# A drain between two stages reordered: probabilities, reciprocals and the first job's rounding

## What is computed

```python
q, k, v = heads(ln(x) @ Wq.T), heads(ln(x) @ Wk.T), heads(ln(x) @ Wv.T + bv)
a = softmax(q @ k.T * 384**-0.5 + adj)            # rows that are all zero give 0
x = x + (a @ v) @ Wo.T + bo
u = ln(x)
logits = u.mean(axis=1) @ router_w.T + router_b   # one choice for each graph
gate = softmax of the two greatest of four logits
h = act_e(u @ w1[e] + b1[e])                      # gelu, silu, mish, gelu
y = sum over the two experts of gate * (h @ w2[e] + b2[e]) + u
x = x + layernorm(y) * ln_g + ln_b
```

## Time and profile before

| what | us |
|---|---|
| median of 3 runs | 1617.83 |
| lowest, highest | 1617.38, 1619.46 |
| the profiled execution, its own time | 1619.34 |
| its span, first to last instruction | 1617.50 |
| TensorE busy | 1586.6 |
| VectorE busy | 1194.9 |
| ScalarE busy | 970.5 |
| GpSimd busy | 687.1 |

### The profile page before, as it was taken

The page is one execution under the profiler, slowest core; times in us unless marked ns, Lnnn a source line. Parts: engine busy times, 40 slices in busy tenths (PEclk is TensorE's granted clock), DMA queues, the critical chain, the costliest instruction groups (busy, mean ns, idle before and its releaser), DMA issues.

```text
span 1617.5 us, 44743 instructions
## 1 busy us (share of the span) xinstructions
PE 1586.6 (98%) x12720; PEld 1524.0 (94%) x12720; DVE 1194.9 (74%) x3754; ACT 970.5 (60%) x2880; POOL 687.1 (42%) x1105
## 2 busy tenths in 40 slices
PE   8999999999999999989999999999999999999998
PEld 7999999999999999879999999999999999999998
DVE  5787788878887778777766666676777767677776
ACT  6899999988999988863433333344344433344442
POOL 3777887778777877731111111111111111111112
PEclk9999999999999999999999999999999999999999
DMA  5433333344444433682211111111111111111211
GB/s 181 161 121 124 104 118 116 130 155 152 155 158 145 152 132 116 211 341 84 60 59 53 56 59 60 56 59 61 61 60 46 60 60 56 60 60 52 67 47 45
DMA packets 93512, 163.87 MB, mean 101 GB/s; under 512 B 10305, under 2 KB 73793, under 8 KB 92097
## 3 DMA queue, kind: packets, MB, share of 16 engines
q1 hardware_dynamic: 91664, 145.01, 27.2%
q10 hardware_dynamic: 1584, 15.73, 2.7%
HBM read 96.22 MB, written 64.49 MB: 99 GB/s over the span
## 4 chain that ended last, share of the span: by engine, by line
PE 89%; DVE 4%; ACT 2%; issue 2%; DMA 1%; DVEq 1%; POOL 0%; ACTq 0%; POOLq 0%; SPq 0%
PE bank L495 69%; PE bank L570 5%; PE bank L709 5%; PE bank L522 3%; PE bank L593 3%; PE bank L610 2%; PE bank L579 1%; PE bank L602 1%; DVE half_t L1458 1%; DVE inverse L1465 1%; DVE inverse L1461 1%; ACT inverse L1009 1%; ACT at_hi L1002 1%; ACT prob L781 1%; DVE hid L1339 0%
## 5 line engine op out<-in xcount | busy, mean ns | idle before, releaser
L495 PE MATMUL bank<-w_hi,ut_in 128*128 x1536 | 421.2, 341 | 0.4 <-issue 0.4
L495 PE MATMUL bank<-w_both,at_hi 128*128 x1524 | 390.0, 336 | 8.7 <-DVE at_lo L1430 8.0
L781 ACT ACTIVATE prob<-att,heads 128x128 f32<-128x128 f32 x768 | 297.5, 393 | 15.3 <-DVE heads L1182 12.3
L495 PEld LDWEIGHTS bank<-w_both,at_hi 128*128 128x128 f32 x1524 | 275.1, 188 | 14.3 <-issue 14.3
L495 PEld LDWEIGHTS bank<-w_hi,ut_in 128*128 128x128 f32 x1536 | 279.5, 188 | 1.4 <-issue 1.4
L495 PE MATMUL bank<-w_lo,ut_in 128*128 x768 | 256.9, 335 | 0.0
L495 PE MATMUL bank<-w_both,at_lo 128*128 x762 | 255.7, 336 | 0.0
L926 ACT ACTIVATE hid<-hid 128x384 f32<-128x384 f32 x192 | 95.1, 526 | 257.2 <-DVE hid L1339 256.5
L1002 ACT ACTIVATE at_hi<-bank,gate_col 128x384 fp32r<-128x384 f32 x254 | 133.4, 576 | 191.0 <-PE bank L709 189.1
L1158 POOL TENSOR_TENSOR xz<-xz,lnb_wide 128x384 f32<-128x384 f32 x64 | 67.6, 1057 | 405.6 <-DVE xz L1496 384.0
L1430 DVE SCALAR_TENSOR_TENSOR at_lo<-bank,gate_col,at_hi 128x384 fp32r<-128x384 f32 x254 | 144.8, 612 | 112.5 <-ACT at_hi L1002 112.5
(11 more groups left out here) (139 smaller groups left out, 3482.3 us busy)
## 6 DMA issues: line engine op xcount, KB each, us to landing
xu_scratch<-xu SPq DMA_DIRECT2D x64, 384.0 KB, 2.3
xz<-xu_scratch SPq DMA_DIRECT2D x64, 384.0 KB, 3.3
x_in<-in_x SPq DMA_DIRECT2D x32, 384.0 KB, 3.3
xu<-in_x SPq DMA_DIRECT2D x32, 384.0 KB, 4.3
ut_scratch<-ut_out SPq DMA_DIRECT2D x64, 192.0 KB, 1.9
ut_in<-ut_scratch SPq DMA_DIRECT2D x64, 192.0 KB, 2.3
out_dram<-xz SPq DMA_DIRECT2D x64, 192.0 KB, 1.9
w_lo<-in_L_ffn_w SPq DMA_DIRECT2D x4, 1152.0 KB, 6.1
```

Of the source, the lines that this page charges most:

```text
L495: last = nc.tensor.matmul(acc, lhs[c][a], rhs[c][b], start=start and n == 0, stop=stop and n == len(terms) - 1)
L781: nc.scalar.activation(prob[g][:, hh, :], att[g][:, head, :], ACT.Exp, bias=neg_max[g][:, head:head + 1], scale=-1.0, accum_out=row_sum[g] ...
```

## The change

In the drain, ScalarE copies one of the three groups of graph 62's probabilities between the exponentials of graph 63, and the reciprocals of graph 62 before the last three of them; VectorE's list loses that copy. TensorE's third group of transposes of graph 63 moves behind the output projection of graph 62. In the expert stage, ScalarE rounds the activation of job (0, 0) before it activates job (0, 1). All work stays, only its place and, for one copy, its engine change; all other steps and jobs are as before.

```diff
--- before.py
+++ after.py
@@ -662,9 +662,10 @@
                     transpose_u(B - 2)
                 if h == B:
 
-                    for c in range(PTC):
-                        transpose_probs(B - 1, c)
+                    transpose_probs(B - 1, 0)
+                    transpose_probs(B - 1, 1)
                     project_o(B - 2)
+                    transpose_probs(B - 1, 2)
                     spread_inverse(B - 1)
                     attend(B - 1)
                 if h < B:
@@ -969,8 +970,11 @@
 
             normalise_x1(B - 4)
             load_under_residuals()
-            exps(B - 1, (0, 1, 2, 3))
+            exps(B - 1, (0,))
+            take_probs(B - 2, 0)
+            exps(B - 1, (1, 2))
             take_inverse(B - 2)
+            exps(B - 1, (3,))
             load_under_scores()
             take_probs(B - 1, 0)
             take_probs(B - 1, 1)
@@ -1021,11 +1025,14 @@
                 for k in range(K):
                     if graph(b, 0):
                         e = choice(b, k)
+                        if isinstance(b, int) and (b, k) == (0, 1):
+
+                            split_act_hi(0, 0, 0)
                         if not isinstance(b, int) or (b, k) != (0, 0):
                             activate(b, k, e)
                     if k == 0 and graph(b, -1):
                         split_act_hi(b - 1, 1, m - 1)
-                    if k == 1 and graph(b, 0):
+                    if k == 1 and graph(b, 0) and not (isinstance(b, int) and b == 0):
                         split_act_hi(b, 0, m)
                     if isinstance(b, int) and (b, k) == (0, 1):
                         take_u(B - 1)
@@ -1399,7 +1406,7 @@
 
             add_bias_and_max(B - 1, (0, 1, 2, 3))
             invert_sums(B - 2)
-            for c in range(PTC):
+            for c in range(1, PTC):
                 take_probs(B - 2, c)
             residual(B - 3)
             divide(B - 2)
```

## The result

The changed kernel takes **1622.11 us** (median of 20 runs, 1620.03 to 1624.19), the kernel before, run beside it, 1618.86 us (20 runs, 1617.33 to 1619.48): 3.25 us more, ratio 1.0020, interval 1.0013 to 1.0027. The profiled execution took 1622.67 us (span 1620.9) against 1619.34. The forecast was 1618.6 us, with 1616.6 to 1621.0 as its range, so the kernel became slower than the range allows, by almost exactly the 0.2% that was called measurable. About 1 us of the gap to the forecast is the median of before itself: 1617.83 from three runs, 1618.86 from twenty. As a difference, +0.8 us was forecast and +3.25 measured. All that follows is about these 2.45 us.

A forecast was written before the change was run, and what follows sets the result against it. TensorE, busy 98% of the span, was taken as the bound, so only its waits could pay. -0.67 + 2.07 = +1.40 us, less 0.35 and 0.2, gave +0.8 with edit C 0: 1617.83 to 1618.6 us, range 1616.6 to 1621.0.

The forecast's parts named there:

- Edit B: Drain, graph 63's last transposes behind project_o(62): transposes, copy and inversion in a row add 2.07 us, passage 1.4 us later.
- Edit C: Expert stage, rounding job (0, 0) first: looks like 2.2 us, counted 0, hidden by w2 and then the Mish chain.
- w2's landing: Last piece of w2 lands at 719.76 us, taken as unchanged within 0.5 us; second layer starts at 720.1 as before.
- Edit A: Drain, ScalarE's copy and reciprocals between exponentials: reciprocals and the rest (L1247 before, L1248 after) come 0.67 us earlier.
- The Mish chain: Job (0, 1)'s activation, L1009 to L1469, ready at 725.91 us before; sets when TensorE's next first layer starts.
- The table load: ScalarE's activation table load in the drain: 1.28 us, ending at 704.6, adds nothing; even 2.66 us leaves the sum standing.
- +0.8 us: Delay of take_u, L1009, sum_nodes and all after: 1.40 at 705 us less 0.35 and 0.2, rounded.
- The 0.35 for the stored ut: ScalarE's idle time before the Mish chain, waiting for a stored ut, absorbs 0.35 us of the 1.40.
- The 0.2: Rounding first uses 0.2 us, between 0 and 0.4, of the 1.51 us ScalarE spent issuing before 715.85.
- Rival 1: Clock drops in new pauses at 704 to 706 or before 726, 1.8 us each: one fall 22%, two 7%.
- Rival 2: Drain follows the earlier reciprocals, inverse not held up by the copy: all 0.67 us earlier, 1617.1 us; 12%.
- rival 3: w2 there all along: second layer 2.2 us sooner with clock kept, at most 4.0 us gained, 1613.8 us; 3%.

The follow-up runs named there:

- changed_again: The changed kernel itself, unaltered, run and profiled once more; +3.09 us against the kernel before.
- order_alone: The kernel before with only the third group of transposes moved behind project_o(62); +2.73 us against the kernel before.
- inverse_first: The changed kernel, but VectorE inverts graph 63's sums before copying its third group of probabilities; +0.69 us against the kernel before.
- pause_filled: The changed kernel with 14 unused matmuls in TensorE's pause ahead of the Mish job's transposes; +2.55 us against the kernel before.
- all_filled: The changed kernel with unused matmuls in three TensorE pauses: 9 ahead of project_o(62), 8 behind the third transposes, 14 ahead of the Mish transposes; +1.69 us against before.
- round_first_alone: The kernel before with only job (0, 0)'s rounding put ahead of job (0, 1)'s activation; +0.44 us against the kernel before.
- order_undone: The changed kernel with TensorE's old order, all three groups of transposes before project_o(62); +0.94 us against the kernel before.
- best: Kernel before with edit A, Mish chain moved ahead, 13 unused matmuls before the w2 wait, take_u between Mish squares, early ut store; -0.54 us against before.
- best_filled: The run best with 6 more unused matmuls ahead of the third group of transposes; -0.50 us against the kernel before.
- drain_alone: The kernel before with only ScalarE's copy and graph 62's reciprocals put between the exponentials; +0.50 us against the kernel before.

## Why the prediction was wrong

**What held.** Edit B's chain: L579 came 1.32 us later by the common measure (+1.40 forecast), at 705.24 in the profile. Edit C gives nothing, since w2 is waited for instead: the second layer starts at 720.63, or 25.37 us behind the first exponential, against 25.48 before, so w2's landing did not move although its last issue came later. Edit A gave what it said at L1248 (0.67 us earlier by the common measure), but only inside the drain. The Mish chain sets (0, 1), with L1476 at +1.40. The table load never mattered: 704.13 + 1.28 = 705.41, and the copy behind it began at 705.83, with its idle time put down to the spreading:

```profile
704.13 1.28 ACT L985 ACT_TABLE_LOAD   x1 [1.53 <-PE bank L570]
705.83 0.49 ACT L812 ACTIVATE inv_t<-bank 128x384 f32<-128x384 f32 x1 [0.41 <-PE bank L579]
```

By the 2.66 us that the Trainium skill (ScalarE: Activation LUTs, section What ACT_TABLE_LOAD costs) gives for a switch with its drain, the copy could not have begun before 706.79 (an estimate: 704.13 + 2.66); the measurement decides. The prediction said that the rows of before can't exclude the 2.66 us. The trace of before does: there the load began 0.02 us after the instruction ahead of it had ended, and the copy behind it at 703.88, which is before 701.49 + 2.66 = 704.15.

**The first failed step: "+0.8 us" for the Mish chain.** It was mis-sized; 1.39 was measured at (0, 1). The two slacks were to absorb 0.35 and 0.2 of 1.40. The 0.35 for the stored ut was used. The 0.2 was not a slack but a loss: ScalarE spent 2.09 us issuing ahead of at_hi, not 1.51. Its chain holds two loads of a value into a register at L904, 0.72 and 0.47 us:

```profile
716.25 0.72 ACTq L904
...
717.54 0.47 ACTq L904
```

at_hi so began 23.08 us behind the first exponential and not at 22.4, and take_u, which was 25.39 behind it before, at 26.81: +1.42. The same loads took 0.08 and 0.47 in changed_again and 0.35 and 0.43 in order_alone. Why they vary is open, but the loss is no single event: the same stretch of issuing took 1.85 us in order_alone, 1.94 in inverse_first, 2.13 in pause_filled and 2.27 in all_filled. The term's error is 0.6 us by the first profile (1.39 for 0.8) and 1.0 by all_filled, which has no fall and stands at +1.82.

**The second, and larger by the timeline: the clock left out of the sum.** Rival 1 named both places, 704 to 706 and 726, and its price of 1.8 us is near the 1.55 measured. But it got 22% and 7% where both profiles of the changed kernel show one fall, and the forecast went by the sum without it. Two sentences were the fault. "It decides once the pause before 726 passes 2.2 us": by my own numbers that pause ran from 723.9 to past 726.3, 2.4 us, so the condition that I had set was met in my own forecast. And "the pause of 1.3 us before project_o(62) did not do it" spoke for one pause, while the changed kernel has two there, 1.78 and 1.50 us with some 2.3 us of work between, and another of 0.39. The length of a pause doesn't settle it in either direction: behind the same pauses of 1.78 and 1.5 us the clock fell in changed_again and not in the first profile, and in order_alone it fell behind none of four, of 1.67, 1.51, 2.09 and 1.14 us. The kernel before shows a fall too, at 721 us; what I should have asked is not whether the clock falls, but whether the fall still lies in front of a wait that hides it. B and C together took away just the wait behind which TensorE's slow layer had been free.

**Added up,** by the timeline of the first profile: 0.8 as forecast, 0.59 more at (0, 1) for the chain, 1.56 for the fall behind it (8.58 - 7.02): 2.95 us at (1, 0), and 2.99 at (2, 1). The median says 3.25, with an interval from some 2.1 to 4.4 us. Rival 2 ("the inverse is not held up by the copy") needed the order that inverse_first then made, and rival 3 is excluded by the waits for w2 in round_first_alone and order_undone.

## What to carry to other kernels

When an edit shortens one wait in a nearly full engine, list what else is ready within the next 2 us (here w2, the Mish chain, b2): each took over in turn, and of all the kernels only best, which moves them all, came to (2, 1) sooner than before, by 0.96 us in its one profile; best_filled, with the same moves, did not. An instruction moved behind another on one engine moves its consumer too, so look at what stands behind the consumer in its list: here the order of two steps in VectorE's list made 0.95 of the 1.3 us that B cost at the first layer. And note for every fall of the clock which wait hides it, and give a forecast the fall as its base case when the edit takes that wait away.

## What I had not expected of the hardware

- In the same kernel the clock fell to 0.50 at 729 us in one execution and at 707 us in another, behind pauses of 2.65 us in the one and 1.78 with 1.51 us in the other, for 3 to 4 us each time; in inverse_first a pause of 1.81 us was followed by a fall. In order_alone none was, with one pause of 2.09 us among them.
- A load of a value into a register of ScalarE took from 0.08 to 0.72 us at the same line.
- SP waited 3.4 us for the last ut's store to land in one kernel and 6.2 us in another (before and drain_alone), and through SP's order that became a wait of VectorE for b2.
- The passage began between 693.08 and 695.26 us in the profiled executions, with the same work ahead of it: 2.2 us, more than any one edit alone moved (2, 1).
